# A four-layer network on one core: the fourth block's chain issued behind its steps' products, and the last stage's variance taken from squares on ScalarE

## The reference, cut to what matters

```python
def _gemma_mlp(x, gate_w, up_w, down_w):
    g = jnp.einsum('bsh,hi->bsi', x, gate_w)
    u = jnp.einsum('bsh,hi->bsi', x, up_w)
    return jnp.einsum('bsi,ih->bsh', jax.nn.gelu(g, approximate=True) * u, down_w)
```

```python
y1 = _ln(x + _mha(x, in_proj_w, in_proj_b, out_proj_w, out_proj_b), ln1_g, ln1_b)
y2 = _ln(y1 + _moe(y1, wg, w1, b1, w2, b2), ln2_g, ln2_b)
```

## Time and profile before

| | us |
|---|---|
| median of 3 runs (lowest, highest) | 1633.42 (1632.73, 1634.76) |
| the profiled execution's own time | 1636.18 |
| its span from first to last instruction | 1634.5 |
| PE busy (share of the span) | 1510.3 (92%) |
| DVE busy | 1072.4 (66%) |
| ACT busy | 450.6 (28%) |
| POOL busy | 461.6 (28%) |
| granted TensorE clock, mean | 0.965 |

### The profile page before, as it was taken

One profiled execution on the slowest core, in us unless ns is written; L12 is line 12 of the kernel. 1 busy time (PEld: TensorE's weight loads), 2 busy tenths in 40 slices (PEclk: granted clock), 3 DMA queues, 4 the chain that ended last, 5 costly groups with the idle time before them and its releaser, 6 DMA issues. The chain is left out here.

```text
span 1634.5 us, 26893 instructions
## 1 busy us (share of the span) xinstructions
PE 1510.3 (92%) x10648; PEld 922.2 (56%) x10648; DVE 1072.4 (66%) x3225; ACT 450.6 (28%) x695; POOL 461.6 (28%) x392
## 2 busy tenths in 40 slices
PE   7999789999999999898979998889999999999882
PEld 3447678888888887443434443344444457544761
DVE  1639889696868746478879667634783398613735
ACT  2333111111111100133323333221112476712442
POOL 0002322323222512356665666600000000000363
PEclk9999789999999999999989999999999999999985
DMA  8910000000000013485556765520142027100235
GB/s 354 240 17 1 2 2 8 2 8 3 9 3 9 3 34 122 139 273 181 170 174 194 251 216 173 174 116 0 51 156 65 0 78 235 36 7 0 75 132 103
DMA packets 91025, 155.93 MB, mean 95 GB/s; under 512 B 42524, under 2 KB 56981, under 8 KB 88853
## 3 DMA queue, kind: packets, MB, share of 16 engines
q1 hardware_dynamic: 68884, 82.91, 15.8%
q0 software_dynamic: 22016, 71.32, 14.7%
HBM read 141.62 MB, written 16.78 MB: 97 GB/s over the span
## 5 line engine op out<-in xcount | busy, mean ns | idle before, releaser
L521 PE MATMUL peer_ps_h<-all_x,layer_down 128*128 128x256 f32 x768 | 182.5, 392 | 0.0
L659 POOL TENSOR_TENSOR peer_bm<-peer_bm,peer_slots 128x512 f32<-128x512 f32 x36 | 109.0, 3028 | 244.8 <-DVE peer_bm L755 244.8
L521 PEld LDWEIGHTS peer_ps_h<-all_x,layer_down 128*128 128x128 f32 x768 | 145.9, 194 | 22.5 <-issue 2.1
L560 PE MATMUL peer_ps_o<-peer_hg,layer_up 128*128 128x256 f32 x640 | 142.3, 380 | 0.2 <-DVE peer_hg L787 0.2
L604 ACT ACTIVATE peer_hg<-peer_ps_h 128x512 f32<-128x512 f32 x96 | 57.3, 597 | 273.6 <-PE peer_ps_h L521 273.6
L560 PEld LDWEIGHTS peer_ps_o<-peer_hg,layer_up 128*128 128x128 f32 x640 | 120.5, 190 | 20.2 <-issue 3.3
L1499 PE MATMUL skills_ps_u<-all_x,skills_w 128*128 128x512 f32 x256 | 122.4, 601 | 8.1 <-DVE skills_hid L1169 4.1
L1444 PE MATMUL skills_acc<-skills_hid,skills_w 128*128 128x512 f32 x256 | 121.9, 600 | 7.0 <-issue 4.5
L1499 PE MATMUL skills_ps_g<-all_x,skills_w 128*128 128x512 f32 x256 | 123.0, 603 | 0.0
L1515 ACT ACTIVATE skills_act_g<-skills_ps_g 128x512 f32<-128x512 f32 x83 | 49.1, 597 | 234.7 <-PE skills_ps_g L1499 185.5
L819 POOL DMA_INDIRECT layer_qw<-expert_rows,all_route x88 | 88.1, 1002 | 52.1 <-issue 24.6
(11 more groups left out here) (457 smaller groups left out, 2621.7 us busy)
## 6 DMA issues: line engine op xcount, KB each, us to landing
four_ring<-in_l_w SPq DMA_DIRECT2D x8, 1024.0 KB, 4.8
quant_w<-in_l_w SPq DMA_DIRECT2D x32, 256.0 KB, 4.3
all_early<-in_l_w SPq DMA_DIRECT2D x26, 256.0 KB, 3.6
skills_w<-in_skills SPq DMA_DIRECT2D x16, 384.0 KB
layer_down<-in_down SPq DMA_DIRECT2D x1, 4096.0 KB, 26.3
layer_up<-in_up SPq DMA_DIRECT2D x1, 4096.0 KB, 35.2
expert_rows<-in_up SPq DMA_DIRECT2D x1, 4096.0 KB, 41.1
four_skill<-in_skills SPq DMA_DIRECT2D x1, 3072.0 KB
```

Source lines behind the costliest of these rows:

```text
L521: mm = pe.matmul(ps_h[group % 2][:, r, :], down[:, c, j * P:(j + 1) * P], g.x[:, c, bass.ds(i * PB, PB)], start=(c == 0), stop=(c == C - 1))
L560: mm = pe.matmul(ps_o[:, c, :], up[:, j, c * P:(c + 1) * P], hg[half][:, j, :], start=(j == 0), stop=(j == NJ - 1))
L659: pool.tensor_tensor(bm[c % RING][:], bm[c % RING][:], slots[half][:, 2, c * PAIRS:(c + 1) * PAIRS].unsqueeze(2).to_broadcast([P, PAIRS, WJ]),
```

## The change

Skills stage, PE's stream: the chain's pieces of steps 65, 66 and 67 stand behind `down(j - 2)` of their step and no longer ahead of its products. Those of steps 70 and 71 stay.

```diff
-                if j == TURN3:
-                    pe.wait_ge(vstep, marks["used", NCH - 1])
-                    pe.wait_ge(hid_done, deep[-1] + 1)
...
-                if j == TURN3 + 1:
-                    pe.wait_ge(block3_step, after["t_done"])
...
-                if j == TURN3 + 2:
-                    pe.wait_ge(block3_step, after["hs_done"])
...
                 if j > 1:
                     down(j - 2)
+                if j == TURN3:
+                    pe.wait_ge(vstep, marks["used", NCH - 1])
+                    pe.wait_ge(hid_done, deep[-1] + 1)
...
+                if j == TURN3 + 1:
+                    pe.wait_ge(block3_step, after["t_done"])
...
+                if j == TURN3 + 2:
+                    pe.wait_ge(block3_step, after["hs_done"])
...
```

```diff
-            pe.wait_ge(presets, 3)
-            pe.wait_ge(vstep, marks["diag"])
...
             for i in range(NPAIR + 3):
                 if i < NPAIR:
                     products(i)
+                if i == 1:
+                    spread_affine()
...
                 if i < NPAIR:
                     deviation(i)
+                if i == 1:
+                    act.wait_ge(spread, 1)
+                    act.activation(affine[:].rearrange("p k d -> p (k d)"), free[0][:], ACT.Copy).then_inc(spread_done, 1)
                 if 0 <= i - 1 < NPAIR:
                     keep_rows(i - 1)
```

```diff
-                if p >= 2:
-                    dve.wait_ge(n2_done, p - 1)
+                if p >= 3:
+                    dve.wait_ge(n2_done, p - 2)
                 for i in range(2):
                     t = 2 * p + i
...
+                    s.did(dve.scalar_tensor_tensor(out=acc[p % 3][:, i, :], in0=held[:, t, :], scalar=weight[:, t:t + 1],
+                                                   in1=y1t[:, t, :], op0=ALU.mult, op1=ALU.add, accum_out=total[:, t:t + 1]))
                 s.settle(dve)
-                for i in range(2):
-                    s.did(dve.bn_stats(stat[:, 1, 2 * p + i, :], acc[p % 2][:, i, :]))
-                s.settle(dve)
-                for i in range(2):
-                    s.did(dve.bn_aggr(mv[:, 1, 2 * p + i, :], stat[:, 1, 2 * p + i, :]))
-                marks["stats", 1, p] = s.n
+                of = slice(2 * p, 2 * p + 2)
+                s.did(dve.tensor_scalar(centre[:, of], total[:, of], -1.0 / D, None, ALU.mult))
+                marks["centre", p] = s.n
...
-            for p in range(NPAIR):
-                mix(p)
-                if p > 0:
-                    give(p - 1)
-                spread2(p)
-            give(NPAIR - 1)
+            for p in range(NPAIR + 2):
+                if p < NPAIR:
+                    mix(p)
+                if 0 <= p - 1 < NPAIR:
+                    spread2(p - 1)
+                if p >= 2:
+                    give(p - 2)
...
+            def measure_rows(p):
+                act.wait_ge(vstep, marks["centre", p])
+                for i in range(2):
+                    t = 2 * p + i
+                    act.activation(squares[:, i, :], acc[p % 3][:, i, :], ACT.Square, bias=centre[:, t:t + 1],
+                                   accum_out=spread_sq[:, t:t + 1]).then_inc(squared, 1)
+                act.wait_ge(squared, 2 * (p + 1))
+                of = slice(2 * p, 2 * p + 2)
+                act.activation(sd[:, 1, of], spread_sq[:, of], ACT.Sqrt, bias=g.eps[:, 1:2], scale=1.0 / D).then_inc(sd_done, 1)
+
+            def normal_rows(p):
                 act.wait_ge(vstep, marks["spread2", p])
                 if p >= 2:
                     act.wait_ge(o_ready, p - 1)
...
+            for p in range(NPAIR + 1):
+                if p < NPAIR:
+                    measure_rows(p)
+                if p > 0:
+                    normal_rows(p - 1)
```

More of the change, by code:

```diff
@@ L2062, in tail @@
         nrm = [sb(f"nrm{i}", [P, 2, D]) for i in range(2)]
-        acc = [sb(f"acc{i}", [P, 2, D]) for i in range(2)]
+        acc = [sb(f"acc{i}", [P, 2, D]) for i in range(3)]
+        squares = sb("squares", [P, 2, D])
+        total = sb("total", [P, NT])
+        centre = sb("centre", [P, NT])
+        spread_sq = sb("spread_sq", [P, NT])
         o = [sb(f"o{i}", [P, C, pair]) for i in range(2)]
@@ L2067, in tail @@
         affine = sb("affine", [P, 2, D])
-        stat = sb("stat", [P, 2, NT, 6])
-        mv = sb("mv", [P, 2, NT, 2])
+        stat = sb("stat", [P, 1, NT, 6])
+        mv = sb("mv", [P, 1, NT, 2])
         sd = sb("sd", [P, 2, NT])
@@ L2102, in tail @@
         n_done, l_done = sem("n_done"), sem("l_done")
[L2103 removed]
+        squared, n2_done, o_ready, o_done = sem("squared"), sem("n2_done"), sem("o_ready"), sem("o_done")
         rows_written = sem("rows_written")
@@ L2336, in spread_offsets, with spread_affine @@
                     mm.then_inc(spread, 1)
+            def spread_affine():
+                pe.wait_ge(presets, 3)
+                pe.wait_ge(vstep, marks["diag"])
+                for k in range(2):
+                    for c in range(C):
+                        mm = pe.matmul(free[0][:, k * D + c * P:k * D + (c + 1) * P], ones[:], diag[:, k, c, :], start=True, stop=True)
+                mm.then_inc(spread, 1)
             def turn_slots(e):
@@ L2365, in give @@
                 mm.then_inc(o_ready, 1)
-            pe.wait_ge(presets, 3)
-            pe.wait_ge(vstep, marks["diag"])
-            for k in range(2):
-                for c in range(C):
-                    mm = pe.matmul(free[0][:, k * D + c * P:k * D + (c + 1) * P], ones[:], diag[:, k, c, :], start=True, stop=True)
-            mm.then_inc(spread, 1)
             for i in range(NPAIR + 3):
@@ L2422, in _ @@
             residual(0)
-            act.wait_ge(spread, 1)
-            act.activation(affine[:].rearrange("p k d -> p (k d)"), free[0][:], ACT.Copy).then_inc(spread_done, 1)
             for i in range(NPAIR + 2):
@@ L2446, in _ @@
                 outcome(e // C, e % C)
-            for p in range(NPAIR):
-                act.wait_ge(vstep, marks["stats", 1, p])
-                act.activation(sd[:, 1, 2 * p:2 * p + 2].unsqueeze(2), mv[:, 1, 2 * p:2 * p + 2, 1:2], ACT.Sqrt,
-                               bias=g.eps[:, 1:2]).then_inc(sd2_done, 1)
+            def measure_rows(p):
[8 more added lines that the diff above has]
+            def normal_rows(p):
                 act.wait_ge(vstep, marks["spread2", p])
@@ L2455, in _ @@
                     t = 2 * p + i
-                    n2 = act.activation(nrm[p % 2][:, i, :], acc[p % 2][:, i, :], ACT.Identity,
+                    n2 = act.activation(nrm[p % 2][:, i, :], acc[p % 3][:, i, :], ACT.Identity,
                                         bias=shift[:, t:t + 1], scale=sd[:, 1, t:t + 1])
                 n2.then_inc(n2_done, 1)
+            for p in range(NPAIR + 1):
[3 more added lines that the diff above has]
+                    normal_rows(p - 1)
         @block.sync
```

27 lines of the change are left out of this document (12 added, 15 removed).

## The result

The changed kernel takes **1627.38 us** (median of 6 runs, 1624.78 to 1629.04). The kernel before, run beside it, takes 1634.96 (6 runs, 1632.73 to 1642.31). The ratio is 0.995, 95% interval 0.9929 to 0.9971: 7.6 us faster. The forecast was 9.3 less than its median, a ratio of 0.9943. The profiled execution of the changed kernel ran 1626.32 us, span 1624.6, against 1636.18 and 1634.5: 9.9 us less.

A forecast was written before the change was run, and what follows sets the result against it. PE, busy 92% of the span, was taken as the bound, with the last loop bound by latency and gathered rows close behind. Median 1633.42 - 8.0 (skills stage) - 1.3 (last loop) = 1624.1 us; range 1620 to 1628.5.

The forecast's parts named there:

- (a): Skills stage, PE: moving the chain of steps 65 to 67 behind the products saves 8.0 us.
- Hole, clock and wait: Skills stage, PE: the saving's three shares, 5.2 us idle hole, 2.3 lower clock, 0.5 wait of L1469.
- The bounds 6.5 and 9: Skills stage saving: 6.5 us if the clock falls in one run in two, 9 if it stayed low longer before.
- The zero for what is late next: Skills stage, behind L1474: no new wait, hidden(68) in time with 0.3 us to spare.
- 1089.82 for the old order: Skills stage, PE: the time in us when step 67's products end in the kernel before.
- (b): Start of the tail's stage: the product for affine moved, gain 0, bounds -0.3 to +0.6 us.
- (c): Tail's last loop: squares on ACT, one pair deeper; 2.4 us sooner against the profile, 1.3 against the median.
- the stutter: Old last loop: shift starts 5.43 us apart instead of 3.48; the extra 1.95 suspected in the profile only.
- The rows do not bind: Last loop: gathers slow only through stores or loop, so an earlier loop gives 5.7 us; total 1620.5; chance 0.12.
- The rows bind harder: Last loop: last rows land 2 to 3 us later, loop ends 1 to 2 later than before; 1627; chance 0.15.
- The waits only move: Skills stage: late hidden(63) makes step 65's up product hold PE until after the gather; about 1631; chance 0.05.
- Slower, by table loads: Last loop, ACT: Square and Sqrt need different tables, two 1.28 us loads a pair; total 1637.5; chance 0.05.

The follow-up runs named there:

- e1_only_a: The kernel before with only the skills part, the chain of steps 65 to 67 moved behind the products; 1627.71 us, ratio 0.9948.
- e9: e8 with step 70's four matmuls that spread the routing weights moved behind its gate and up products; 1626.53 us, ratio 0.994.
- e3: The kernel before with only the tail's new last loop, squares on ScalarE and one pair deeper; 1635.17 us, ratio 0.9997.
- e4: The whole change as it is, all three parts, measured again beside its parts; 1628.93 us, ratio 0.9955.
- e7: The changed kernel with four output buffers o instead of two, so give waits for older stores; 1624.73 us, ratio 0.9947.
- e6: The changed kernel with a zero row of its own for each token without a place; 1621.6 us, ratio 0.9935.
- e11: e8 with one 3 us memset on POOL ahead of the last four gathers; 1623.94 us in one run.
- e12_held: e9 with POOL waiting for DVE's centre(5) before issuing the gathers of the last two pairs; 1622.57 us, ratio 0.993.
- e8: The changed kernel with both own zero rows and four output buffers o; 1623.43 us, ratio 0.9947.
- e10: e8 with 32 tiny memsets on DVE ahead of the last loop; 1627.57 us in one run.

## Why the prediction was right, and where it was not

**(a), 8.0 forecast.** 8.1 in the pair of profiles; 7.5 for the region as a mean of three against three, and 8.6 by the medians of e1_only_a. Hole, clock and wait came out by themselves: idle 5.65 to 0.45; the clock 2.4 in the mean (forecast 2.3); L1469's 0.33 with its issue. The bounds 6.5 and 9 were about right, for another reason than the one given: not the clock's chance but the length of the hole, 3.9 to 5.65, which depends on how late the expert rows bring `down(62)`. In e1 the gather had ended before PE came. The zero for what is late next held: `hidden(68)` was in time, and nothing new was late. But the barrier's was not PE's only later wait, as the prediction had it: the earlier trace rows begins at 1123 and leaves out 1.2 us in step 70 and 0.4 in step 72, which both kernels have. They keep their distance to their steps, as it said, and e9 shows that the first could go too. Its 1089.82 for the old order was 0.1 short of the trace; the same 0.1 stands behind L1502 in the new one, so the difference is not touched.

**(b), 0 forecast, -0.3 to +0.6.** From the stage's start to the first `mix`, the profiles with the same slow stretches give 85.68, 85.54 and 85.60 without (b) and 84.93, 85.52, 85.36, 85.43, 85.68 and 85.68 with it: 0.2 less in the mean, within their spread. The 2.2 by which the first part of the tail was longer in the changed kernel's profile is not (b): e1_only_a, without it, has them too.

```profile
1511.60:1597.30 85.70, 73.18 (x388) 60.85 (x388) 42.31 (x211) 36.17 (x73) 43.31 (x42) 0.86 0.30 102
```

The row of e1's stretch has the same 0.86 of clock and the same length. It is the profile of before that was lucky in its clock, and it gave back there what it had lost near 1253.

**(c), 2.4 against the profile, 1.3 against the median.** The profile's 2.4 came out as 1.85, and old loops (32.43, 32.41, 32.28, 32.21) against new (30.58, 29.87, 30.63) as 2.0. The costs were right: `mix` with its centre 1.1 (forecast 1.25), two squares with reads 1.1, the root 0.30, no table load behind the first. **The step that failed is the reading of the stutter.** The prediction took the 0.94 idle on DVE for a thing of that one execution ("so I suspect that the 1.95 are in the profile only") and cut 2.4 to 1.3. It is in all four profiles of the old loop, and a stop that ends at the same time after the first `mix` is in the new one: 1.73 here, 0.8 to 1.5 in e3, e4 and e7, and 3.9 to 4.2 where the rest is fast. That the two are one thing is likely and not shown.

**Two terms were left out behind the rows.** The forecast let the loop end 7.0 us after the landing of the last rows. That is what it did wherever the rows set `mix(7)`: 6.97 in e3_only_c and 6.93 in e7_o4_after. In the changed kernel's profile `mix(6)` still started 0.31 behind its rows, but `mix(7)` 2.04 behind, since `give(4)` ahead of it came late. `give(4)`, at its new pace, came back to its tile before the store had left it, which the prediction priced at nothing: of its 2.12 idle, 0.88 lie behind the end of PE's transposes, the other thing it needs. The rest is what is left of the stop ahead of centre(5), whose squares stand ahead of `nrm(4)` on ACT; this is argued from the order of the stream and not tested alone. The rows came 21.9 after the first `mix` and not 23.0. So 30.0 was forecast for the loop and 30.6 came out by two errors that nearly cancel, 1.1 too late for the rows and about 1.6 too little behind them: that much is luck.

**The rivals.** *The rows do not bind* was priced at 5.7 for the loop. Its mechanism, gathers slow by what the stores or the loop do, is wrong: they were as slow in the shorter loop, and e6 shows the shared row as the cause. With the rows made fast (e6, e8) the loop gave 2.4 to 2.8, since the stop stood behind them, and 4.7 in e11, where the stop was gone too. *The rows bind harder*: they landed 21.9 after the first `mix`, 22.8 before; no, though they held `mix(5)` by 2.08. *The waits only move*: no. *Slower, by table loads*: one load of 1.28, not sixteen; no. The Trainium skill (ScalarE: Activation LUTs, Table sets: the hidden batching unit) does not name Square among the functions of every set. The trace shows it running with the table of the Exp, which was loaded 40 us earlier, and with that of the root, and the one load is followed within 0.02 by the next instruction. The Trainium skill (Vector Engine (DVE) Microarchitecture Reference, Points that are easy to get wrong) gives half throughput for such a `mix`. The trace does not agree: two operations start 0.41 apart with both operands in SBUF.

**The total.** 9.3 forecast, 7.6 measured with an interval of 4.7 to 11.6: (a) nearly in full, and of (c) nothing that a median of this kernel can show.

## What to carry to other kernels

A chain between two engines belongs behind work that does not need it; its worth is the idle time plus what the clock loses behind it, and both can be read off one timeline. When a stall in a loop has no releaser, look for it in a second profile before calling it chance: this one was in all twelve profiles in which POOL's work around it was not moved, and it took most of what faster rows gave. And filler indices of a gather should not all name one row: here their packets became up to four times slower, though no gain of the whole kernel is shown from mending it.

## What was not expected of the hardware

- Where many indices of the gathers named one row of HBM, the packets of 4096 bytes of a pair took up to 0.70 us in the median; with a row for each they took 0.16 to 0.18 (e6_zero_after).
- A DVE operation of 128x2, normally 0.17 us, lasted 2.43 us beside a memset on POOL and ended with it (e11_late, centre(4)), though `mix` operations of 256 columns ran just before, beside the same memset.
- DVE stops 0.8 to 4.2 us ahead of one small instruction, `shift(4)` in the old loop and centre(5) in the new one, always ending 17.5 to 18.8 us after the first `mix`, and not when POOL's last gathers come later (e11_late, e12_held). Its cause was not found.
- The granted clock of the tail's first part differs between executions of the same work: 0.86 over 85.5 us for most, 0.89 over 83.3 for the kernel before, 0.81 over some 89 for e9, e11 and e12. e6 took 89.5 us too, at 0.85. All four have the rows of zeros of their own, but so have e8 and e10 with 85.7, so the edit alone does not decide it. These 3.5 us are more than (b) and (c) together.
